# The routing stage of a language-model tower: quads of tiles in a software pipeline, row-wise passes on ScalarE

## The reference, cut to what matters

```
x      = layernorm(h)                          # per token, over 128 numbers
logits = x @ router_w + router_b               # 64 experts
probs  = softmax(logits)
top_w, top_idx = top_k(probs, 42)
top_w  = softmax(top_w)
comb   = zeros(tokens, 64); comb[token, top_idx] = top_w
out    = sum over e of comb[:, e] * (gelu(x @ w1[e] + b1[e]) @ w2[e] + b2[e])
```

## Time and profile before

| | us |
|---|---|
| median of 3 runs (2108.2 to 2109.22) | 2108.68 |
| the profiled execution, whole | 2107.91 |
| its span in the trace | 2106.2 |

### The profile page before, as it was taken

One profiled execution on the slowest core, in us unless ns is written; L12 is line 12 of the kernel. 1 busy time (PEld: TensorE's weight loads), 2 busy tenths in 40 slices (PEclk: granted clock), 3 DMA queues, 4 the chain that ended last, 5 costly groups with the idle time before them and its releaser, 6 DMA issues.

```text
span 2106.2 us, 30090 instructions
## 1 busy us (share of the span) xinstructions
PE 1880.2 (89%) x8406; PEld 1454.3 (69%) x8406; DVE 1878.0 (89%) x2448; ACT 1443.6 (69%) x2560; POOL 734.2 (35%) x472
## 2 busy tenths in 40 slices
PE   5408977777765999999999999999999999999998
PEld 3303435555544788888888888878888888888887
DVE  8536788888868799999999999979999999999997
ACT  2105546666622788888888888878888888888886
POOL 5350335445411233333333333323333333333330
PEclk9958558999965999999999999999999999999999
DMA  6410000000012233333333333323333333333331
GB/s 196 141 40 1 0 0 1 1 0 0 1 28 92 90 119 124 124 124 120 111 117 124 124 124 121 113 90 124 124 124 124 113 114 123 124 124 124 114 112 57
DMA packets 104084, 191.27 MB, mean 91 GB/s; under 512 B 12390, under 2 KB 85078, under 8 KB 87382
## 3 DMA queue, kind: packets, MB, share of 16 engines
q1 hardware_dynamic: 101998, 186.64, 25.9%
q0 software_dynamic: 2048, 4.20, 0.7%
HBM read 179.27 MB, written 11.53 MB: 91 GB/s over the span
## 4 chain that ended last, share of the span: by engine, by line
PE 66%; DVE 0%; issue 0%; ACT 0%; DVEq 0%; ACTq 0%
PE f_ps_h L1795 11%; PE f_ps_h L1796 11%; PE f_ps_h L1797 11%; PE f_ps_y L1806 11%; PE f_ps_y L1808 11%; PE f_ps_y L1807 11%; PE f_ps_y L1821 0%; DVE s_lo L1751 0%; DVE scaled L1745 0%; PE f_ps_h L1832 0%; ACT act_out L1706 0%; DVE h L1769 0%; ACT y_t L1730 0%; DVEq L1627 0%; PE f_ps_h L1777 0%
## 5 line engine op out<-in xcount | busy, mean ns | idle before, releaser
L1706 ACT ACTIVATE act_out<-f_ps_h,b_t 128x512 f32<-128x512 f32 x1024 | 649.5, 686 | 257.6 <-PE f_ps_h L1797 257.6
L1745 DVE TENSOR_TENSOR scaled<-act_out,c_row 128x1024 f32<-128x1024 f32 x512 | 753.7, 1472 | 42.9 <-ACT act_out L1706 39.6
L1751 DVE TENSOR_TENSOR s_lo<-scaled,s_hi 128x1024 fp32r<-128x1024 f32 x512 | 672.7, 1314 | 0.1
L1714 ACT ACTIVATE s_hi<-scaled 128x1024 fp32r<-128x1024 f32 x512 | 542.1, 1059 | 2.3 <-DVE scaled L1745 1.6
L1609 POOL CAST w_hi<-w_raw 128x512 fp32r<-128x512 f32 x128 | 201.8, 1576 | 909.1 <-PE f_ps_y L1808 897.3
L1795 PE MATMUL f_ps_h<-x_hi,w_hi 128*128 x1024 | 399.8, 390 | 2.1 <-DVE h L1769 1.5
L1806 PE MATMUL f_ps_y<-s_hi,w_hi 128*128 128x512 f32 x1024 | 398.9, 390 | 3.0 <-DVE s_lo L1751 3.0
L1796 PE MATMUL f_ps_h<-x_lo,w_hi 128*128 x1024 | 399.3, 390 | 0.0
L1797 PE MATMUL f_ps_h<-x_hi,w_lo 128*128 x1024 | 399.1, 390 | 0.0
L1808 PE MATMUL f_ps_y<-s_hi,w_lo 128*128 128x512 f32 x1024 | 398.4, 389 | 0.0
L1807 PE MATMUL f_ps_y<-s_lo,w_hi 128*128 128x512 f32 x1024 | 398.4, 389 | 0.0
(11 more groups left out here) (211 smaller groups left out, 1762.9 us busy)
## 6 DMA issues: line engine op xcount, KB each, us to landing
c_row<-comb_rows SPq DMA_DIRECT2D x128, 1024.0 KB, 4.9
w_raw<-in_w SPq DMA_DIRECT2D x256, 128.0 KB, 4.3
by_slot<-b_zeros SPq DMA_DIRECT2D x1, 3072.0 KB, 13.6
b_gauss_s<-by_slot SPq DMA_DIRECT2D x12, 256.0 KB, 5.1
mixed_rows<-b_mixed SPq DMA_DIRECT2D x12, 256.0 KB, 2.3
out<-h SPq DMA_DIRECT2D x8, 256.0 KB, 4.8
cent<-in_centers SPq DMA_DIRECT2D x1, 1536.0 KB
neg_prec<-in_logvar SPq DMA_DIRECT2D x1, 1536.0 KB
```

What stands on the lines that cost most here:

```text
L1706: last = act.activation(act_out[:, r % 2, c, :], ps_h[:, r % 2, c, :], ACT.Gelu, bias=b1_t[:, c, bass.ds(e, 1)])
L1714: act.activation(s_hi[:, r % RING], scaled[:, r % RING], ACT.Copy).then_inc(hi_ready, 1)
L1745: dve.tensor_tensor(scaled[:, r % RING], act_out[:, r % 2], c_row[:, k, g * GT:(g + 1) * GT].unsqueeze(1).broadcast_to([P, HC, GT]), ALU.m ...
L1751: dve.tensor_tensor(s_lo[:, r % RING], scaled[:, r % RING], s_hi[:, r % RING].bitcast(F32), ALU.subtract).then_inc(lo_ready, 1)
```

## The change

In `route` alone:

- `norm` moves from DVE to ACT: four activations a quad, Identity with `rstd` as scale and a new `shift` (minus mean times `rstd`, made once on DVE) as bias.
- DVE no longer makes `d1` and `d2`: ACT's exponentials run tile by tile with `neg_max` and `neg_r1` as bias, the first one straight from PSUM with its sum as a second output. DVE's sum over the quad becomes one pass over 4 numbers that negates the sums.
- The product `comb` moves to ACT: `weigh`, four activations with `r2` as scale.
- An exponential of one column is put ahead of everything, after the root.
- All loops over quads are written out, the buffers between DVE and ACT are double, and the engines' orders are new: DVE takes `maximum(q + 1)`, `choose(q)`, `probabilities(q + 1)`; ACT and PE as in the diff.

The diff, without the new buffers' declarations, POOL's loop, and `copy_x`, `copy_comb`, `turn_x` and `turn_comb`, which keep their instructions and get their buffer from `q % 2`:

```diff
+            act.activation(warm[:], shifted[:, 0:1], ACT.Exp, scale=0.0)
+
+            def norm(q):
                 if in_range(q, QUADS):
-                    hold(act, comb_turned, q + 1)
-                    act.activation(comb_t[:, cols(q)], ps_c[0:EXPERTS, b], ACT.Copy).then_inc(comb_copied, 1)
-
-            def step(q, b):
-                copy_x(q, b)
-                act.wait_ge(d1_ready, q + 1)
-                act.activation(e1[:], d1[:], ACT.Exp).then_inc(exp_one, 1)
-                copy_comb(q - 1, 1 - b)
-                act.wait_ge(d2_ready, q + 1)
-                act.activation(e2[:], d2[:], ACT.Exp, scale=-1.0).then_inc(exp_two, 1)
-
-            repeat(act, step, QUADS)
-            copy_comb(QUADS - 1, 1)
+                    act.wait_ge(ln_ready, 1)
+                    after(act, turned, q - 1)
+                    for k in range(QT):
+                        t = q * QT + k
+                        last = act.activation(xn[:, q % 2, k, :], h[:, t, :], ACT.Identity, scale=rstd[:, t:t + 1],
+                                              bias=shift[:, t:t + 1])
+                    last.then_inc(normed, 1)
...
+            def first_exps(q):
+                if in_range(q, QUADS):
+                    b = q % 2
+                    act.wait_ge(max_ready, q + 1)
+                    for k in range(QT):
+                        last = act.activation(e1[:, b, k, :], ps_l[:, b, k * EXPERTS:(k + 1) * EXPERTS], ACT.Exp,
+                                              bias=neg_max[:, b, k:k + 1], accum_out=s1[:, b, k:k + 1])
+                    last.then_inc(exp_one, 1)
+
+            def second_exps(q):
+                if in_range(q, QUADS):
+                    b = q % 2
+                    act.wait_ge(p_ready, q + 1)
+                    for k in range(QT):
+                        last = act.activation(e2[:, b, k, :], neg_p[:, b, k, :], ACT.Exp, scale=-1.0,
+                                              bias=neg_r1[:, b, k:k + 1])
+                    last.then_inc(exp_two, 1)
+
+            def weigh(q):
+                if in_range(q, QUADS):
+                    b = q % 2
+                    act.wait_ge(r2_ready, q + 1)
+                    after(act, comb_turned, q - 1)
+                    for k in range(QT):
+                        last = act.activation(comb[:, b, k, :], top[:, b, k, :], ACT.Copy, scale=r2[:, b, k:k + 1])
+                    last.then_inc(comb_ready, 1)
...
+            norm(0)
+            norm(1)
+            copy_x(0)
+            first_exps(0)
+            second_exps(0)
+            for s in range(QUADS + 2):
+                copy_x(s + 1)
+                first_exps(s + 1)
+                copy_comb(s - 2)
+                weigh(s - 1)
+                second_exps(s + 1)
+                norm(s + 2)
...
-            dve.reciprocal(rstd[:], root[:]).then_inc(rstd_ready, 1)
-            dve.wait_ge(rstd_ready, 1)
-
-            def norm(q, b):
+            dve.reciprocal(rstd[:], root[:]).then_inc(ln_step, 1)
+            dve.wait_ge(ln_step, 1)
+            dve.scalar_tensor_tensor(out=shift[:], in0=mv[:, :, 0], scalar=-1.0, in1=rstd[:], op0=ALU.mult,
+                                     op1=ALU.mult).then_inc(ln_ready, 1)
+
+            def maximum(q):
                 if in_range(q, QUADS):
-                    after(dve, turned, q - 1)
-                    for k in range(QT):
-                        t = q * QT + k
-                        last = dve.tensor_scalar(xn[:, b, k, :], h[:, t, :], mv[:, t, 0:1], rstd[:, bass.ds(t, 1)],
-                                                 ALU.subtract, ALU.mult)
-                    last.then_inc(normed, 1)
-
-            def probabilities(q, b):
-
-                of_quad = ps_l[:, b, 0:QT * EXPERTS].rearrange("p (k e) -> p k e", k=QT)
-                link = chained(dve, sum_step, q * 3)
-                dve.wait_ge(logits, q + 1)
-                dve.tensor_reduce(neg_max[:], of_quad, AX.X, ALU.max, negate=True).then_inc(max_ready, 1)
-                hold(dve, max_ready, q + 1)
-                dve.tensor_tensor(d1[:], of_quad, spread(neg_max), ALU.add).then_inc(d1_ready, 1)
-                norm(q + 1, 1 - b)
-                dve.wait_ge(exp_one, q + 1)
-                link(dve.tensor_reduce(neg_s1[:], e1[:], AX.X, ALU.add, negate=True))
-                link(dve.reciprocal(neg_r1[:], neg_s1[:]))
-                link(dve.tensor_tensor(neg_p[:], e1[:], spread(neg_r1), ALU.mult))
-                dve.tensor_tensor(d2[:], neg_p[:], spread(neg_r1), ALU.subtract).then_inc(d2_ready, 1)
-
-            def choose(q, b):
-
+                    b = q % 2
+                    dve.wait_ge(logits, q + 1)
+                    dve.tensor_reduce(neg_max[:, b], ps_l[:, b, 0:QT * EXPERTS].rearrange("p (k e) -> p k e", k=QT),
+                                      AX.X, ALU.max, negate=True).then_inc(max_ready, 1)
+
+            mark_p, settle_p, link_p = chain(dve, p_step, 0)
+
+            def probabilities(q):
+                if in_range(q, QUADS):
+                    b = q % 2
+                    dve.wait_ge(exp_one, q + 1)
+                    link_p(dve.scalar_tensor_tensor(out=neg_s1[:], in0=s1[:, b], scalar=-2.0, in1=s1[:, b], op0=ALU.mult,
+                                                    op1=ALU.add))
+                    link_p(dve.reciprocal(neg_r1[:, b], neg_s1[:]))
+                    dve.tensor_tensor(neg_p[:, b], e1[:, b], spread(neg_r1[:, b]), ALU.mult).then_inc(p_ready, 1)
...
+                settle()
                 dve.wait_ge(exp_two, q + 1)
-                link(dve.scalar_tensor_tensor(out=top[:], in0=left[:], scalar=MARK, in1=e2[:], op0=ALU.is_gt,
+                link(dve.scalar_tensor_tensor(out=top[:, b], in0=left[:], scalar=MARK, in1=e2[:, b], op0=ALU.is_gt,
                                               op1=ALU.mult))
-                link(dve.tensor_reduce(s2[:], top[:], AX.X, ALU.add))
-                link(dve.reciprocal(r2[:], s2[:]))
-                after(dve, comb_turned, q - 1)
-                dve.tensor_tensor(comb[:, b], top[:], spread(r2), ALU.mult).then_inc(comb_ready, 1)
-
-            def step(q, b):
-                if not isinstance(q, int) or q > 0:
-                    hold(dve, comb_ready, q)
-                probabilities(q, b)
-                choose(q, b)
-
-            ROUNDS = -(-DROPPED // 8)
-            STEPS = 2 * (2 * ROUNDS + 1) + 3
-            norm(0, 0)
-            repeat(dve, step, QUADS - 2)
-            for q in (QUADS - 2, QUADS - 1):
-                step(q, q % 2)
+                link(dve.tensor_reduce(s2[:], top[:, b], AX.X, ALU.add))
+                dve.reciprocal(r2[:, b], s2[:]).then_inc(r2_ready, 1)
+
+            maximum(0)
+            probabilities(0)
+            for q in range(QUADS):
+                maximum(q + 1)
+                after(dve, comb_ready, q - 1)
+                choose(q)
+                probabilities(q + 1)
...
+            def logit(q):
+                if in_range(q, QUADS):
+                    b = q % 2
+                    pe.wait_ge(x_copied, q + 1)
+                    after(pe, exp_one, q - 1)
+                    for k in range(QT):
+                        of_tile = ps_l[:, b, k * EXPERTS:(k + 1) * EXPERTS]
+                        pe.matmul(of_tile, x_s[:, b, k * P:(k + 1) * P], rw[:], start=True, stop=False)
+                        last = pe.matmul(of_tile, ones_row[:], rb[:], start=False, stop=True)
+                    last.then_inc(logits, 1)
...
-            def step(q, r):
-                turn_x(q, r % 2)
-                logit(q, r % 2)
-                turn_comb(q - 1, (r - 1) % 2)
-
-            repeat(pe, step, QUADS, 4)
-            turn_comb(QUADS - 1, 1)
+            turn_x(0)
+            logit(0)
+            turn_x(1)
+            for s in range(QUADS + 1):
+                logit(s + 1)
+                turn_x(s + 2)
+                turn_comb(s - 1)
```

More of the change, by code:

```diff
@@ L1341, in route @@
         root = sb("r_root", [P, TILES])
+        shift = sb("r_shift", [P, TILES])
+        warm = sb("r_warm", [P, 1])
         xn = sb("r_xn", [P, 2, QT, DIM])
         x_s = sb("x_s", [P, 2, GT])
-        neg_max = sb("r_neg_max", [P, QT])
-        d1 = sb("d1", [P, QT, EXPERTS])
-        e1 = sb("e1", [P, QT, EXPERTS])
+        neg_max = sb("r_neg_max", [P, 2, QT])
+        e1 = sb("e1", [P, 2, QT, EXPERTS])
+        s1 = sb("s1", [P, 2, QT])
         neg_s1 = sb("neg_s1", [P, QT])
[L1348 to L1351, removed]
+        neg_r1 = sb("neg_r1", [P, 2, QT])
+        neg_p = sb("neg_p", [P, 2, QT, EXPERTS])
+        e2 = sb("e2", [P, 2, QT, EXPERTS])
         left = sb("left", [P, QT, EXPERTS])
         low = sb("low", [P, QT, 8])
-        top = sb("top", [P, QT, EXPERTS])
+        top = sb("top", [P, 2, QT, EXPERTS])
         s2 = sb("s2", [P, QT])
-        r2 = sb("r2", [P, QT])
+        r2 = sb("r2", [P, 2, QT])
         comb = sb("comb", [P, 2, QT, EXPERTS])
@@ L1363, in route @@
         rooted = sem("r_rooted")
```

(89 more changed lines are left out.)

1 line of the change is left out of this document (added).

## The result

The changed kernel takes 2148.99 us (median of 4 runs, 2147.07 to 2150.36) against 2108.72 us (median of 4 runs of the kernel before, 2108.2 to 2109.22); the ratio is 1.019, 95% interval 1.0177 to 1.0203. The forecast was 2149.

A forecast was written before the change was run, and what follows sets the result against it. DVE was taken to bound the routing stage before; in the new order a serial wait of 9.44 us plus DVE's 6.37 makes a 15.81 us quad. The stage grows 40.35 us, giving 2149 us, range 2141 to 2160.

The forecast's parts named there:

- Who waits for whom: Routing stage, new engine lists: norm(q+1) stands behind second_exps(q) on ACT, choose(q) behind maximum(q+1) on DVE, so logits run bare.
- What bounded the kernel before: Routing stage before: DVE bounds it, 9.96 us a quad, with PE's logits of the next quad made beside it.
- the upper end of its range: Whole kernel: 2160 us, with no overlap on ACT and DVE losing 9.96 - 8.95 seven times.
- The wait: DVE in a steady quad, from the end of neg_p to the next maximum: six links summing to 9.44 us.
- DVE's own part: DVE in a steady quad, from maximum to the end of neg_p: 6.37 us of work, against 8.95 before.
- turn_comb hidden: PE between copy and logits: turn_comb(q-1) fits in the gap, some 1.8 us against 1.78, so it costs nothing.
- Start: Start of the routing stage: second table load of 1.28 us, maximum(0) at 605.77, 1.54 us later than before.
- Whole stage: Routing stage from start through quads 1 to 7 to the end: 40.35 us longer than before.
- The granted clock: Rival: PE at its 2.4 GHz level in the routing stage instead of 0.50, time 2125 us; chance 0.04.
- Identity: Rival: ACT's Identity in norm brings a table load a quad, 9 us more, time 2158 us; chance 0.05.
- The pipelining rival: Rival: logit(q+1) ready when DVE reaches maximum(q+1), PE sets a quad of 7.19 us, time 2091.5 us; chance 0.04.

The follow-up runs named there:

- Each swap: Two runs on the changed kernel: norm(s + 2) ahead of second_exps(s + 1) on ScalarE, 1.0108; choose(q) ahead of maximum(q + 1) on DVE, 1.0079 of the kernel before.
- the deeper order: Changed kernel with transposes, copies and logits one quad further ahead, same instructions and buffers: 0.9915 of the kernel before.
- the one written out: Kernel before with repeat(...) replaced by a plain loop on every engine, same work and order: 0.9989 of the kernel before.
- both versions further ahead: Changed kernel with transposes, copies and logits one quad further ahead, 0.9915; the same with one 256-column bias matmul a quad, 0.9895 of the kernel before.

## Why the prediction was right

- **Who waits for whom** held. It needed no duration: follow one quad's semaphores through the four ordered lists, and the next quad's logits begin behind this quad's `neg_p`. Each swap took away about the part of the wait that follows from it, and the deeper order nearly all.
- **What bounded the kernel before** was put too simply: DVE's work is 8.95 of a mean quad of 9.96. The rest was in part a wait for logits (0.51 ahead of quad 1), in part the loop, and one microsecond POOL's splitting beside DVE in the seventh quad. In the changed kernel the splitting falls into DVE's wait and lengthens nothing. The forecast didn't use this rest but for the upper end of its range.
- **The wait, 9.44 us forecast, was 9.54.** The links: second exponentials to `norm` 0.97 (0.96), `norm` 1.63 (1.57), transposes to copy 1.15 (1.13), copy to logits 0.65, logits to maximum 5.04. The per-row operand priced from a copy's rows was right: two of them make 0.478 each, by the mean of L1417; the forecast was 0.475.
- **DVE's own part, 6.37, was 6.26** (623.55 - 617.29). The small passes start sooner behind each other: the pass over 4 numbers is 0.13 long and starts 0.09 after the reciprocal. The two errors cancel in 15.81 against 15.80.
- **turn_comb hidden**: the copy-to-logits gap stayed 0.65, with turn_comb in it from quad 3 on. By the diff this is `turn_comb(q - 2)`, where the prediction wrote `turn_comb(q - 1)`; both are four transposes, so the sum is the same.
- **Start.** Maximum(0) came at 608.00 - 596.31 = 11.69 after the stage's start, forecast 605.77 - 594.21 = 11.56; before it was 10.02. The root ended at 597.84, the second table load ran from 597.85 to 599.13, and its activation started at 599.15. The Trainium skill, ScalarE: Activation LUTs, What ACT_TABLE_LOAD costs, adds a drain of some 1.38 us to each switch; this trace shows none on either side of the load:

```profile
597.85 1.28 ACT L1409 ACT_TABLE_LOAD   x1
...
599.15 0.20 ACT L1409 ACTIVATE r_warm<-r_shifted 128x1 f32<-128x1 f32 x1
599.26 3.17 ACT L1417 ACTIVATE r_xn<-h,r_shift,rstd 128x128 f32<-128x128 f32 x8
```

- **Whole stage**: 40.35 forecast, 40.3 measured. That the median also met 2149 within a tenth is partly luck: single runs lie 3 us apart, and this profiled execution had 2.1 us from elsewhere.
- **Rivals.** The granted clock stayed 0.50. Identity brought no table load: ACT has two in the stage, both at its start, which agrees with the Trainium skill, ScalarE: Activation LUTs, Table sets: the hidden batching unit. The pipelining rival came true once its condition was made: with the logits ready the kernel fell to 0.9915 of the time before. Its price, 2091.5 or 0.992, fits that version, in part by luck: PE's quad was 6.73 and not 7.19, which is 3 us less over the stage, but DVE also waited 3.07 for the logits of quad 1, and its seventh quad took 7.71, with two passes at 1.19 and 1.17 beside POOL's splitting of weights.
- **What the forecast didn't have**: the logits' 5.0 us contain 1.1 us for having product and bias in turn. It didn't matter for the sum, which took them whole from a row, but it did for the first expectation of the kernel without a bias.

## What to carry to other kernels

A software pipeline over in-order engines is as deep as its worst list: before anything is timed, follow the next item's chain through every engine's list, and ask at each wait what stands behind it that doesn't need it. Here the next quad's `norm` and copy behind the second exponentials on ScalarE, and `choose` behind the maximum on VectorE, turned some 2.7 us less of DVE's work a quad into a loss of 5.8. Either swap alone took away only a part. Having ScalarE and PE one quad further ahead, without a new instruction and with VectorE's list as it was, turned it back. To see whether a stretch of work is bare or hidden, remove the same piece in both kernels and compare.

## What the runs showed of the hardware

At the granted clock of 0.50, the 1.2 GHz level, small fp32 matmuls that contract over 128 rows and over 1 row in turn, into the same columns, started 0.31 us apart; in groups of one shape they started 0.22 to 0.24 apart, 5.00 against 3.87 us for the same sixteen. One bias matmul of 256 columns was 1.22 us long, where a group of four of 64 columns took 1.97:

```profile
628.10 1.97 PE L1571 MATMUL ps_l<-rw,x_s 128*128 128x64 f32 x8 [0.54 <-ACT x_s L1428]
...
629.99 1.22 PE L1572 MATMUL ps_l<-rb,ones_row 1*128 1x256 f32 x2
```

Why the order in turn costs, by the shapes or by adding to columns just written, no run tells.

Passes of DVE that read two tensors of 256 numbers a partition took 0.90 to 1.39 us while POOL split weights beside them, and 0.42 otherwise. It happened in one quad of the kernel before, of the one written out and of both versions further ahead. The sum over `top` in the same stretch kept its 0.42.
